# A group's fold in two parts on TensorE, and the division behind an add on VectorE, in a relative-position attention kernel

## The reference

```
AC   = einsum('bhid,bhjd->bhij', q + u_bias, k)
BD   = rel_shift(einsum('bhid,hjd->bhij', q + v_bias, r @ Wr.T))
attn = softmax((AC + BD) * scale)
out  = einsum('bhij,bhjd->bhid', attn, v)
```

## Time and profile before

| | |
|---|---|
| median of 3 runs | 3015.8 us (3013.68 to 3016.17) |
| the profiled execution | 3010.06 us |
| its span, first to last instruction | 3008.3 us |
| mean granted TensorE clock | 0.975 |
| busy: TensorE, VectorE, ScalarE, GpSimd | 95%, 87%, 83%, 77% |

### The profile page before, as it was taken

One profiled execution on the slowest core, in us unless ns is written; L12 is line 12 of the kernel. 1 busy time (PEld: TensorE's weight loads), 2 busy tenths in 40 slices (PEclk: granted clock), 3 DMA queues, 4 the chain that ended last, 5 costly groups with the idle time before them and its releaser, 6 DMA issues.

```text
span 3008.3 us, 101339 instructions
## 1 busy us (share of the span) xinstructions
PE 2872.3 (95%) x40768; PEld 2021.2 (67%) x40768; DVE 2614.0 (87%) x5002; ACT 2511.6 (83%) x3878; POOL 2319.8 (77%) x4151
## 2 busy tenths in 40 slices
PE   6776999999999999999999999999999999999986
PEld 3552677767776776777777777677777767777755
DVE  5781899989998998989998999999999989999877
ACT  4555889889988988888988988888988988989962
POOL 5558788888887888888888888888888888888850
PEclk8895999999999999999999999999999999999998
DMA  6468888888888888888888888888888888888761
GB/s 226 159 193 220 207 231 224 223 226 228 231 226 223 227 229 223 227 224 225 231 228 225 229 228 222 235 219 225 231 228 221 232 225 227 232 225 223 213 202 57
DMA packets 290228, 656.76 MB, mean 218 GB/s; under 512 B 189536, under 2 KB 256992, under 8 KB 272352
## 3 DMA queue, kind: packets, MB, share of 16 engines
q0 software_dynamic: 190960, 526.89, 66.5%
q1 hardware_dynamic: 98800, 123.38, 13.6%
HBM read 77.19 MB, written 46.14 MB: 41 GB/s over the span
## 4 chain that ended last, share of the span: by engine, by line
PE 81%; POOL 6%; DVE 4%; DMA 4%; ACT 3%; issue 2%; DVEq 0%; SPq 0%; ACTq 0%; POOLq 0%
PE pt_bank L1096 27%; PE acc_bank L1110 17%; PE ac_bank L1082 16%; PE pos_bank L1030 13%; POOL score L898 6%; DMA score<-score 3%; PE pos_bank L1068 3%; PE bank_one L477 2%; ACT score L1157 1%; DVE rest L620 1%; DVE normed_one L152 1%; PE bank_two L262 0%; PE bank_one L448 0%; PE bank_two L251 0%; DVE x_one_sb L227 0%
## 5 line engine op out<-in xcount | busy, mean ns | idle before, releaser
L898 POOL DMA_DIRECT2D score<-score x3999 | 2178.3, 548 | 465.6 <-ACT score L1159 397.0
L1157 ACT COPY score<-pos_bank 128x512 f32<-128x512 f32 x2048 | 1103.5, 596 | 245.7 <-PE pos_bank L1030 243.6
L1167 ACT ACTIVATE score<-score,low 128x1024 f32<-128x1024 f32 x1024 | 1197.9, 1170 | 22.6 <-DVE low L1227 22.6
L1236 DVE COPY prob_t<-pt_bank 128x512 f32<-128x512 f32 x1768 | 1146.5, 683 | 3.6 <-PE pt_bank L1096 3.6
L1096 PEld LDWEIGHTS pt_bank<-ident_sb,score 128*128 128x128 f32 x8192 | 946.7, 142 | 214.1 <-issue 119.1
L1096 PE MATMUL pt_bank<-ident_sb,score 128*128 128x128 f32 x8192 | 1079.3, 274 | 5.0 <-ACT prob_t L1175 1.3
L1227 DVE CUSTOM_DVE_ANT_0 score<-ac_bank,score 128x1024 f32<-128x1024 f32 x512 | 626.9, 1224 | 243.9 <-DMA score<-score 120.6
L1227 DVE CUSTOM_DVE_ANT_0 score<-ac_bank,score,low 128x1024 f32<-128x1024 f32 x512 | 657.2, 1284 | 47.6 <-PE ac_bank L1082 37.5
L1110 PE MATMUL acc_bank<-prob_t,vs 128*32 128x128 f32 x16384 | 659.8, 279 | 0.0
L1030 PE MATMUL pos_bank<-pos,qv 96*32 96x512 bf16 (+15 forms) x12160 | 655.4, 316 | 3.7 <-ACT score L1157 2.5
L1082 PE MATMUL ac_bank<-ks,qu 96*128 96x512 bf16 x2048 | 622.7, 386 | 34.0 <-DVE low L1227 33.8
(11 more groups left out here) (97 smaller groups left out, 855.7 us busy)
## 6 DMA issues: line engine op xcount, KB each, us to landing
score<-score POOLq DMA_DIRECT2D x3937, 129.5 KB, 5.1
pos<-pos_parts SPq DMA_DIRECT2D x96, 128.0 KB, 8.6
qv<-qv_parts SPq DMA_DIRECT2D x192, 64.0 KB, 7.3
ks<-k_parts SPq DMA_DIRECT2D x192, 64.0 KB, 7.2
qu<-qu_parts SPq DMA_DIRECT2D x192, 64.0 KB, 7.4
v_heads<-v_sb SPq DMA_DIRECT2D x8, 1024.0 KB, 6.1
vs<-v_heads SPq DMA_DIRECT2D x32, 256.0 KB, 8.2
pos_parts<-part SPq DMA_DIRECT2D x16, 384.0 KB, 2.7
```

The source lines that it names most:

```text
L898: pool.dma_start(shifted(odd, s, groups, 0), shifted(odd, s, groups, QUAD - 1 - s))\
L1157: act.copy(score[:, at + f, c * BANK:(c + 1) * BANK], ring(m)[:, :]).then_inc(pos_out, 1)
L1167: act.activation(cols, cols, ACT.Exp, bias=low[:, slot(k), NH - 1:NH], scale=-1.0)\
L1236: dve.tensor_copy(prob_t[:, c, :], PT[c % 2][:, :]).then_inc(copied, 1)
```

## The change

TensorE's `fold` of four matmuls is split. `fold_first` keeps the waits and does tiles 0 and 1 of the group at the old place, the end of half A. `fold_rest` does tiles 2 and 3 and raises `fin_full`; it stands at the end of half B. On VectorE, `finish` goes from in front of `add(k+2, 1)` to behind it.

```
-                def fold(step, k):
+                def fold_first(step, k):
...
-                    for f in range(FT):
+                    fold_tiles(range(0, FT // 2))
+
+                def fold_tiles(tiles):
+
+                    for f in tiles:
                         last = pe.matmul(POS[FOLD_AT % 3][:, f * VW:(f + 1) * VW],
                                          lhsT=acc_sb[:, f * P:(f + 1) * P], rhs=fold_sb[:, :], start=True, stop=True)
-                    last.then_inc(fin_full, 1)
+                    return last
+
+                def fold_rest(step, k):
+
+                    fold_tiles(range(FT // 2, FT)).then_inc(fin_full, 1)
...
                         if h and k % FT == 1 and group_there(step, fold_no(k)):
-                            fold(step, k)
+                            fold_first(step, k)
+                        if h == 0 and k % FT == 2 and group_there(step, fold_no(k)):
+                            fold_rest(step, k)
...
                     for h in range(NH):
+                        if h and there(step, n):
+                            add(step, n, 1)
                         if h and k % FT == 2 and group_there(step, fold_no(k)):
                             finish(step, k)
-                        if h and there(step, n):
-                            add(step, n, 1)
                         for c in (2 * h, 2 * h + 1):
```

## The result

The change made the kernel slower, by half of what was forecast: 3030.84 us median (5 runs, 3024.81 to 3034.37) against 3015.8 (5 runs, 3012.0 to 3020.06), ratio 1.0048, 95% interval 1.0032 to 1.0063, 15 us. The profiled execution took 3024.81 us with a span of 3023.0, 14.7 more than before, at the same mean granted clock, 0.975.

A forecast was written before the change was run, and what follows sets the result against it. TensorE, busy 95% of the span, bounds the kernel. A 0.32 us longer group in 123 groups gives +39 us, less 8 coming back: +31 on 3015.8, so 3047 us; own range 3034 to 3063, widened to 3024 to 3067.

The forecast's parts named there:

- The wait of item 6 for the division: Half C: TensorE stands 0.39 us at item 6 of positions for fin_used; a group gets 0.32 us longer, in 123 groups.
- The split's price for TensorE: Fold in two parts, each 0.36 us to turn: between -0.06 and +0.04 us a group; -0.06 taken.
- the fourth rival: TensorE's second fold start costs up to 0.39 us, no wait is seen: 3049 us; chance 0.04.
- the prediction's lowest sum: Content of half A to content of half C with all low ends: 5.90 us, +0.21 a group.
- 0.85 where a fold follows it: VectorE's add behind the content of half B starts 0.85 us after it; 0.74 kept as low end.
- Its matmuls start 0.10 later: TensorE at item 6: matmuls start 0.10 us after its weight load, the content 0.55 after that.
- What comes back: VectorE's 49 waits for shifted rows get 0.32 us more time each: 0 to 16 us back, 8 taken.
- The hidden wait (1): Item 6 does not wait for fin_used, only the split counts: 3008 to 3021, call it 3013 us; chance 0.10.
- the faster kernel (2): Late groups lose the division's 0.43 us in front of the add: 22 us gained, 2994 us; chance 0.07.
- The third: Copy of chunk 2 late for the next turn, delaying adds: stall 0.6 us a group, 3078 us; chance 0.06.

The follow-up runs named there:

- The kernels without late rows: Kernel before, the change, fold split 1+3, fold split 0+4, each with 8 of 31 row shifts per group left out: 2980.77, 3000.44, 2973.64, 2981.87 us.
- the split alone: The change with the division put back in front of the add, against the kernel before: 3027.68 us, ratio 1.0041.
- a kernel with the shortest typical group: The change with one fold tile in half A and three in half B, against the kernel before: 3021.55 us, ratio 1.0018.

## Why the prediction was right in kind and wrong in size

**Right: the place.** The wait of item 6 for the division, in 123 groups, with VectorE's add in front of it; a chain from the content of half B over add, division, item 6 to the content of half C. The split's price for TensorE too: 0.37 from a part to the turn where 0.36 was read, content of half B at 2.82 where 2.81 was forecast. The second part's first weight load, on PEld of the kernel after, starts 0.23 us behind the start of a content whose record ends at 1515.73:

```profile
1515.35 0.63 PEld L1072 LDWEIGHTS pos_bank<-fold_sb,acc_sb 128*128 128x128 f32 x4
```

It did not wait for the content to end, and the fold follows its content by 0.44 us in both parts, so the fourth rival has nothing for it. (The rule of the Trainium skill, page "TensorE: Matmul & The Clock Gate", Part 3, that a load overlaps running matmuls only with another row group, would have had it wait; the measurement decides. The same Part lets a load go ahead of running matmuls too where it is for the background weight buffer; this row would agree with that, but which buffer the load went to no run here shows.)

**Wrong: two terms of that chain, 0.21 us in all, so that 0.32 was forecast and 0.13 came.** (Two other steps came out 0.01 longer each than they were read, so the sum was 0.19 off.) The first was taken at the high of two readings; the second had no low end at all, so that even the prediction's lowest sum, +0.21, lay above what came.

1. "0.85 where a fold follows it ... so I take 0.85". It measured 0.74 (1515.12 to 1515.86), with a fold part right behind. The 0.85 of the earlier trace rows has nothing to do with the fold. It belongs to the first add of a group: in all fourteen traces that add, where it waits for its content, starts 0.85 behind it, and the others that wait for their content 0.74 or 0.75. In the code it alone has two more waits in front, for the two DMA semaphores. The kernel with the fold whole in half B shows that the fold has no part in it: no fold behind the content of half A, and the first add still 0.85 behind it. Its PE and then its DVE:

```profile
1511.54 0.60 PE L1082 MATMUL ac_bank<-ks,qu 96*128 96x512 bf16 x2
```

```profile
1512.39 1.23 DVE L1227 CUSTOM_DVE_ANT_0 score<-ac_bank,score 128x1024 f32<-128x1024 f32 x1 [0.64 <-PE ac_bank L1082]
```

The code shows the difference; that the two waits are what costs is read from it, and no run takes them out. I matched two rows by what came behind them and not by what stood in front.

2. "Its matmuls start 0.10 later". The lead of a weight load over its matmul is seen while TensorE is busy. When it has been let go, load and matmul start together: 1517.56 both. The trace before had it already, in the content of the earlier trace rows. Its weight load stands here, and both start at 627.04.

```profile
627.04 0.11 PEld L1082 LDWEIGHTS ac_bank<-ks,qu 96*128 96x128 bf16 x2 [2.03 <-DVE low L1227]
```

With both set right: 2.82 + 2.44 + 0.56 = 5.82, the measured value. Over 122 groups 0.13 makes 16 us. The median lies inside the range put down, 3024 to 3067, but in the part that was added below 3034 for more coming back. Less came back, so that it lies there is luck.

**What comes back** was forecast at 8 us of at most 16. VectorE's waits for late rows did get shorter: without the first, 104.5 - 57.6 = 46.9 us in 36 waits, where there had been 70.5 in 49 and, in the second trace of the kernel before, 61.9 in 48. But the excess went from 19.8 or 17.1 (two traces of the kernel before) to 17.4, thus by at most 2.4 us, which is less than the two traces of one kernel differ. The kernels without late rows say the same: there the change costs 17.0 us in 122 groups (19.7 by the medians), with late rows 13.3 to 16.1 (15.0), so that 1 to 5 us came back. The prediction priced a late group by its shorter wait alone. The change also moves two tiles of fold out of the place where they were free in a late group: lateness fell from 35.6 or 32.1 us to 24.9, but 0.55 of it reached the groups instead of 0.44 to 0.47. For three and four tiles moved the same effect is far above the noise; for the two of the change it is small enough to be partly chance.

**The rivals.** The hidden wait (1) and the faster kernel (2) did not come: `head_out` is waited for in all but one of the 123 groups. The third did not either, the copy of chunk 2 is in time with the change; in the split alone it is the very wait. The sum forecast +31; the two mis-sized terms took 0.19 x 123 = 23 off, and the smaller share coming back put some 6 to 8 on: about 15, as measured.

## What to carry to other kernels

Before an instruction is moved behind another, list who waits for its semaphore and how much time that waiter has to spare: here 1.41 us, and the move used up a little more than all of it, on an engine that has no idle time to make it up. A duration between two instructions can belong to what stands in front of the waiting one, its other waits included; look for the same latency in a second place before taking the higher. And work that seems to be in the way on the bounding engine may be cover for a delay that comes now and then: a kernel with the shortest typical group was not the fastest until the delays were taken away.

## What the runs showed of the hardware

- TensorE, when it waited for another engine, starts load and matmul at once, 0.06 us after the releasing instruction's end (1517.28 + 0.22 to 1517.56; a turn in the split alone 0.03 behind its load); a stall in the matmuls is therefore shorter than in the loads: 0.17 against the 0.26 that the timeline gives for the load.
- An add with two further waits in front, for DMAs, starts 0.85 us behind its content, one without 0.74 or 0.75, in every trace. In the same way the multiplication of every fourth group, with one further wait for a store, starts 0.28 us behind its reciprocal instead of 0.21. A further wait for a semaphore that VectorE raises itself (`added`, in front of every add with h = 1) costs nothing that can be seen: 0.74 with it, 0.75 without. That it is the waits is read from the code; no run leaves them out.
- The start differs by the execution alone: the first wait for shifted rows was 50.1 and 62.5 us in two traces of one kernel, and the first copy of `ACC` started at 328.0 and 334.5 us.
